# Attention: the split of the maxima moved ahead of the pieces' subtraction on GpSimd, their transposes a step earlier, and the loops written out

## The reference, cut to what matters

```python
x = x + 0.5 * ffn(layernorm(x))        # 8 experts, one for each token, with a capacity
x = x + attn(layernorm(x))             # the part that the change is in
x = x + 0.5 * ffn(layernorm(x))

def attn(x):                           # 16 heads of 8 numbers, causal
    q, k, v = split(sn_dense(x, W_qkv), 3)
    att = where(causal == 0, big_neg, einsum('bhqd,bhkd->bhqk', q, k) * hd ** -0.5)
    att = softmax(att, axis=-1)
    x = einsum('bhqk,bhkd->bhqd', att, v)
    return sn_dense(x, W_proj)
# ffn: num = x @ waff.T (the router's product), softmax, argmax and rank choose the
# expert; then gelu(x @ W1 + b1) @ W2 + b2 of that expert
```

## Time and profile before

| | |
|---|---|
| median of 3 runs | 1170.29 us (1165.38 to 1170.43) |
| the profiled execution's own time | 1164.83 us |
| its span, first to last instruction | 1163.0 us |
| granted clock of TensorE, mean | 0.875 of full speed |
| turns 0 to 31 of the attention | from about 376 us to about 885 us of the span |
| one pass of the loop, four turns | 63.9 us |

### The profile page before, as it was taken

The page is one execution under the profiler, slowest core; times in us unless marked ns, Lnnn a source line. Parts: engine busy times, 40 slices in busy tenths (PEclk is TensorE's granted clock), DMA queues, the critical chain, the costliest instruction groups (busy, mean ns, idle before and its releaser), DMA issues. The chain is left out here.

```text
span 1163.0 us, 28246 instructions
## 1 busy us (share of the span) xinstructions
PE 913.6 (79%) x8020; PEld 690.2 (59%) x8054; DVE 708.6 (61%) x2090; ACT 591.6 (51%) x1538; POOL 721.1 (62%) x1170
## 2 busy tenths in 40 slices
PE   2485638999936899999999999999984455988776
PEld 1374218999923566666666566656552134977776
DVE  6487954444326577777777777777753983434331
ACT  3023415666612566666666666666662433654543
POOL 4261976444132677677776777777652596777775
PEclk9655558999967999999999999999996556999998
DMA  5261002222216455544555544455410001212121
GB/s 163 82 170 43 0 8 66 66 69 67 51 46 119 88 105 117 117 103 105 107 108 117 109 103 104 107 116 115 98 40 10 1 0 38 52 51 53 48 50 30
DMA packets 124656, 88.51 MB, mean 76 GB/s; under 512 B 13649, under 2 KB 115078, under 8 KB 124566
## 3 DMA queue, kind: packets, MB, share of 16 engines
q1 hardware_dynamic: 101782, 52.36, 20.1%
q0 software_dynamic: 8960, 18.14, 6.6%
q10 hardware_dynamic: 13824, 16.92, 6.6%
HBM read 52.23 MB, written 34.87 MB: 75 GB/s over the span
## 5 line engine op out<-in xcount | busy, mean ns | idle before, releaser
L1379 DVE TENSOR_REDUCE at_mx<-at_pp 128x2 f32<-128x512 f32 (+1 forms) x384 | 259.8, 686 | 80.0 <-PE at_pp L1233 68.9
L1165 ACT ACTIVATE at_pt<-at_pm 128x512 f32<-128x512 f32 x384 | 224.4, 598 | 150.1 <-PE at_pm L1244 81.3
L1108 POOL TENSOR_SCALAR_AFFINE_SELECT at_pt<-at_pt 128x256 f32<-128x256 f32 (+1 forms) x384 | 182.1, 490 | 125.9 <-ACT at_pt L1165 121.5
L855 ACT ACTIVATE e_ht<-e_ps_h,b1t 128x128 f32<-128x128 f32 x576 | 164.8, 372 | 120.5 <-PE e_ps_h L883 120.4
L817 POOL DMA_INDIRECT e_x<-rows,gidx x144 | 139.0, 965 | 94.5 <-DVE e_y L935 48.3
L883 PE MATMUL e_ps_h<-e_xnt,e_w1own 128*128 128x128 f32 x1152 | 158.1, 282 | 27.8 <-issue 22.7
L883 PEld LDWEIGHTS e_ps_h<-e_xnt,e_w1own 128*128 128x128 f32 x1152 | 144.2, 197 | 31.9 <-issue 31.9
L893 PE MATMUL e_ps_y<-w,e_ht 128*128 x1152 | 159.7, 282 | 0.0
L893 PEld LDWEIGHTS e_ps_y<-w,e_ht 128*128 128x128 f32 x1152 | 140.5, 192 | 1.7
L1244 PE MATMUL at_pm<-qs,kb 128*128 128x256 bf16 x512 | 97.7, 272 | 29.0 <-ACT at_pt L1165 26.2
L935 DVE SCALAR_TENSOR_TENSOR e_y<-e_ps_y,e_x 128x256 f32<-128x256 f32 x72 | 30.6, 425 | 143.2 <-PE e_ps_y L893 143.2
(11 more groups left out here) (256 smaller groups left out, 1626.2 us busy)
## 6 DMA issues: line engine op xcount, KB each, us to landing
at_qkd<-at_part SPq DMA_DIRECT2D x64, 192.0 KB, 3.0
kb<-at_qkd SPq DMA_DIRECT2D x64, 96.0 KB
qs<-at_qkd ACTq DMA_DIRECT2D x64, 96.0 KB
x<-e_y SPq DMA_DIRECT2D x36, 128.0 KB, 1.8
rows<-ts_x ACTq DMA_DIRECT2D x16, 264.0 KB, 3.0
rows<-at_x SPq DMA_DIRECT2D x32, 132.0 KB
ts_x<-in_x_dram SPq DMA_DIRECT2D x16, 256.0 KB, 3.2
x_by_token<-at_xa SPq DMA_DIRECT2D x32, 128.0 KB
```

Source lines behind the costliest of these rows:

```text
L855: last = a.activation(hid_t[j % NB][:, f, :], ps_h[j % NB][:, f, :], ACT.Gelu, bias=c.b1t[:, ds(e, 1), f])
L1108: g.affine_select(out=tile, in_=tile, compare_op=ALU.is_ge, fill=0.0, base=0, pattern=[[0, n], [1, P]], channel_multiplier=-1).then_inc(ma ...
L1165: a.activation(pt[u % RING][:, :], pm[u % 2], ACT.Exp, scale=SCALE).then_inc(exped, 1)
L1379: v.tensor_reduce(out, src, axis=AX.X, op=ALU.max).then_inc(maxed, 1)
```

## The change

It has three parts.

1. On GpSimd, in step 5, the four operations that cut the maxima of sequence b+1 come ahead of the subtraction for sequence b+3; before, they came behind it.
2. On TensorE the maxima are turned in step 7 instead of step 8, and the router's product is made in step 8 instead of step 7. ScalarE's copies follow: the turned maxima in step 7 and the router's numbers in step 8. The waits on the shared bank are changed to match: the transposes wait for the product of the turn before, and the product waits for the copy of the turned maxima.
3. All turns of the attention and all steps of `token_stats` are written out. The loops go, and with them the registers and the increments of a semaphore `passed`.

The diff, cut to its core:

```diff
-        def turns(turn):
-            for b in range(-4, NQ):
-                turn(b, b % NQ, lambda o, b=b: 0 <= b + o < B)
-            yield
-            for b in range(B - NQ, B + 2):
-                turn(b, b % NQ, lambda o, b=b: 0 <= b + o < B)
-            yield
-        def run(eng, turn):
-            emit = turns(turn)
-            next(emit)
-            with eng.Fori(1, B // NQ - 1) as i:
-                for k in range(NQ):
-                    turn(i * NQ + k, k, lambda o: True)
-            next(emit)
+        def run(turn):
+            for b in range(-4, B + 2):
+                turn(b, b % NQ, lambda o, b=b: 0 <= b + o < B)
...
 # GpSimd, step 5
+                    if u == 5 and has(1):
+                        n, q = b + 1, (k + 1) % 2
+                        wait(pool, maxed, (n + 1) * NP)
+                        flat = mx[q][:, :, :, :].rearrange("p j r g -> p j (r g)")
+                        g.tensor_copy(mp[q][:, :, 0, :], flat).then_inc(cuts, 1)
...
+                        g.tensor_tensor(mp[q][:, :, 2, :], nr[q][:, :, :], mp[q][:, :, 1, :], ALU.subtract).then_inc(mp_done, 1)
                     if u == 5 and has(3):
                         q = (k + 1) % 2
                         wait(pool, b_done, b + 4)
                         g.tensor_tensor(part[q][:, 2:4, :], rest[q][:, :].rearrange("p (a n) -> p a n", a=2), part[q][:, 1:5:3, :],
                                         ALU.subtract).then_inc(part_done, 1)
-                    if u == 5 and has(1):
-                        n, q = b + 1, (k + 1) % 2
-                        wait(pool, maxed, (n + 1) * NP)
...
 # ScalarE
-                    if u == 7 and has(-2):
-                        wait(act, num_mm, b - 1)
...
-                    if u == 8 and has(1):
+                    if u == 7 and has(1):
                         q = (k + 1) % NQ
                         wait(act, mt_tr, b + 2)
...
+                    if u == 8 and has(-2):
+                        wait(act, num_mm, b - 1)
...
 # TensorE
-                    if u == 7 and has(-2):
-                        wait(pe, x2t_out, b - 1)
-                        wait(pe, v_out, b + 4, B)
...
+                    if u == 7 and has(1):
+                        wait(pe, mp_done, b + 2)
+                        wait(pe, v_out, b + 4, B)
+                        wait(pe, num_out, b - 2)
...
+                    if u == 8 and has(-2):
+                        wait(pe, x2t_out, b - 1)
+                        wait(pe, mt_out, b + 2, B)
...
-                    if u == 8 and has(1):
-                        wait(pe, mp_done, b + 2)
-                        wait(pe, v_out, b + 4, B)
-                        wait(pe, num_out, b - 1)
```

More of the change, by code:

```diff
@@ L361, in wait, with run @@
         def wait(eng, s, n):
-            if not isinstance(n, int) or n > 0:
+            if n > 0:
                 eng.wait_ge(s, n)
[L366 to L374, removed]
+        def run(step):
+            for b in range(NB):
+                step(b, b % NX, b == 0, b == NB - 1)
         @blk.sync
@@ L378, in load @@
             def load(b, k, first, last):
-                if not isinstance(b, int) or b >= NX:
+                if b >= NX:
                     sp.wait_ge(x_out[k], (b - k) * (16 // NX))
-                    sp.sem_inc(passed, 1)
                     sp.wait_ge(xn_done, (b - (NX - 1)) * TS)
-                    sp.sem_inc(passed, 1)
                     sp.wait_ge(xnorm_done, b - (NX - 1))
-                    sp.sem_inc(passed, 1)
                 sp.dma_start(x_row[k][:, :, 0:D], x_v[:, ds(b, 1), :, :]).then_inc(x_in[k], 16)
-            run(sp, load)
+            run(load)
         @blk.gpsimd
@@ L404, in roots @@
                 g.tensor_tensor(c.xnorm[:, ds(b * TS, TS)], x_row[k][:, :, D + 1], x_row[k][:, :, D + 2], ALU.mult).then_inc(xnorm_done, 1)
-            run(pool, roots)
+            run(roots)
         @blk.scalar
@@ L424, in step @@
                     numbers(b, k)
-            run(act, step)
+            run(step)
             for k in range(NX):
@@ L459, in step @@
                 norm(b, k)
-            run(dve, step)
+            run(step)
         @blk.tensor
@@ L482, in step @@
                     project(b, k)
-            run(pe, step)
+            run(step)
 def consts(nc, m):
@@ L1018, in wait @@
         def wait(eng, s, n, most=None):
[L1020 to L1024, removed]
+            n = n if most is None else min(n, most)
+            if n > 0:
+                eng.wait_ge(s, n)
         def dma_count(b, slots, each=1):
@@ L1085, in turn @@
                     sp.dma_start(row_v[:, ds(b - 2, 1), :, :], x2[k % 2][:, :, :]).then_inc(row_out[k % 2], 16)
-            run(sp, turn)
+            run(turn)
             for k in range(2):
@@ L1130, in turn @@
                         g.tensor_tensor(c.xnorm[:, ds(n * TPB, TPB)], x2[q][:, :, D + 1], x2[q][:, :, D + 2], ALU.mult).then_inc(xnorm_done, 1)
+                    if u == 5 and has(1):
[3 more added lines that the diff above has]
+                        g.tensor_copy(mp[q][:, :, 0, :], flat).then_inc(cuts, 1)
+                        wait(pool, cuts, n * 3 + 1)
+                        g.tensor_tensor(nr[q][:, :, :], flat, mp[q][:, :, 0, :], ALU.subtract).then_inc(cuts, 1)
+                        wait(pool, cuts, n * 3 + 2)
+                        g.tensor_copy(mp[q][:, :, 1, :], nr[q][:, :, :]).then_inc(cuts, 1)
+                        wait(pool, cuts, n * 3 + 3)
+                        g.tensor_tensor(mp[q][:, :, 2, :], nr[q][:, :, :], mp[q][:, :, 1, :], ALU.subtract).then_inc(mp_done, 1)
                     if u == 5 and has(3):
@@ L1151, in turn @@
                         g.tensor_tensor(xa[k % 2][:, :, D + 1], vare[k % 2][:, :], mhalf[:, :], ALU.pow).then_inc(rstd1, 1)
-            run(pool, turn)
+            run(turn)
         @blk.scalar
@@ L1211, in turn @@
                             act.dma_start(qs[q][to:to + size, :, :], src[48 * r:48 * r + size, :, :]).then_inc(qk_in[q], 16)
-            run(act, turn)
+            run(turn)
         @blk.tensor
@@ L1272, in small @@
                         wait(pe, xn_done, (b + 4) * TPB)
[L1273 to L1275 removed]
+                        wait(pe, num_out, b - 2)
+                        wait(pe, v_out, b + 3)
                         for j in range(TPB):
@@ L1307, in small @@
                         last.then_inc(otr, 1)
+                    if u == 7 and has(1):
+                        wait(pe, mp_done, b + 2)
+                        wait(pe, v_out, b + 4, B)
+                        wait(pe, num_out, b - 2)
+                        for j in range(TPB):
+                            last = te.transpose(mi[0].bitcast(BF16)[0:3 * H, j * P:(j + 1) * P],
+                                                mp[(k + 1) % 2][:, j, :, :].rearrange("p t h -> p (t h)"), c.identb[:, :])
+                        last.then_inc(mt_tr, 1)
+                    if u == 8 and has(-2):
+                        wait(pe, x2t_out, b - 1)
+                        wait(pe, mt_out, b + 2, B)
+                        for j in range(TPB):
+                            last = te.matmul(mi[0][:, j * E:(j + 1) * E], x2t[k % 2][:, j * P:(j + 1) * P], c.waff_t[:, :],
+                                             start=True, stop=True)
+                        last.then_inc(num_mm, 1)
                     if u == 7 and has(-1):
@@ L1339, in turn @@
                     small(u)
-            run(pe, turn)
+            run(turn)
         @blk.vector
@@ L1422, in turn @@
                         statistics(b - 1, x2[q], bn2[q], vare2[q], bnd2, mv2, var2, True)
-            run(dve, turn)
+            run(turn)
 def macaron(nc, io, out):
```

35 lines of the change are left out of this document (2 added, 33 removed).

## The result

The changed kernel takes 1203.45 us (median of 4 runs, 1194.41 to 1207.01), the kernel before 1168.74 us (4 runs, 1165.38 to 1170.43). The ratio is 1.0286 with an interval of 1.0257 to 1.0316: slower by 34.7 us. The forecast was 1200 us, with +32.6 us against the profiled execution. Profile against profile it is 1203.77 - 1164.83 = +38.9 us; the span is 1201.7 us.

The account below looks back on a forecast made before the run. The prediction took a circle through GpSimd's subtraction and the landing of `at_qkd` as the bound; +36.0 + 0 - 0.7 - 6.7 + 4 + 0 = +32.6 us gave 1197.4 us, or 1202.9 by the median; it said 1200, range 1186 to 1210.

Parts of the forecast that it names:

- The circle through the subtraction: Attention turn, 15.98 us: GpSimd's queue, subtraction, `at_qkd` flight, ScalarE's transfers, exponential and TensorE's tile by key, without slack.
- The cuts at full price: GpSimd step 5: cuts ahead delay the subtraction by 1.20 us in each of 30 turns, +36.0 us.
- TensorE's new waits at 0: TensorE steps 7 and 8: waits of 0.6 us a turn fit in the room; 18 us if not, chance 6%.
- Writing out at -6.7 us: Attention loop: written-out turns last 15.70 instead of 15.98 us, over 24 turns, mostly from SyncE's register work.
- The last turns at -0.7: Turns 30 and 31: earlier transfer of the turned maxima wins 0.5 to 1 us together, taken as -0.7.
- Fetches at +4 us: Written-out turns: instruction fetches meet some `at_qkd` flights at 0.4 us each, +4 us, bounds 0 and +10.
- The clock: TensorE: its clock would still be granted in full, and its longer wait costs nothing.
- two bases: Whole kernel: 1197.4 us from the profiled execution and 1202.9 us by the median of the runs.
- The signs named beforehand: Profile after: subtractions near 17.0 us apart, flight 3.6 to 4.0, TensorE's wait near 2 or split, ScalarE's gap about 1 longer.
- The rule on taken branches: Loop's five jumps back would each stall engines for a fetch, so writing out is preferred; the sum was left unchanged.

Follow-up runs that it names:

- spare operations: Kernel before plus four unused GpSimd operations of the cuts' size each turn: ratio 1.000 placed behind subtraction and cuts, 1.032 placed ahead of the subtraction.
- part 1 with filler: Kernel before with only the cuts moved ahead of the subtraction, in the loop, plus five extra TensorE products in step 0 of each turn: ratio 1.035.
- both moves: Kernel before with the cuts ahead of the subtraction and the maxima turned in step 7, product in step 8, loops kept: ratio 1.032.
- the cuts behind: Changed kernel with GpSimd's order as before, subtraction first, still written out and maxima turned in step 7: ratio 1.016.
- part 3 alone: Kernel before with all turns written out, cuts still behind the subtraction and maxima turned in step 8: ratio 0.998.
- part 1 alone: Kernel before with only the four cuts moved ahead of the subtraction, loops kept: ratio 1.061.
- the spare operations ahead: Kernel before plus four unused GpSimd operations of the cuts' size ahead of the subtraction each turn, cuts still behind it: ratio 1.032.

## Why the prediction was right, and which of its terms were off

**The circle through the subtraction** is right. It was read from two engines that start on different work at one moment. The spare operations show that the place in GpSimd's queue decides, and part 1 with filler that a later subtraction alone costs its delay.

**The cuts at full price.** Forecast 1.20 us a turn; the block measures 1.10 in the written-out kernel, and in the loop the turn grew by 1.24 (both moves) and 1.11 (spare operations). Right. For the turn ahead of turn 0 the first exponential came 1.4 us earlier in the span instead of 1.2 later, since the attention began 2.3 us earlier; the cost was there (+0.9) but a gain in the written-out stages ahead, which I had put at 0, covered it.

**TensorE's new waits at 0.** Right where the cuts come first: the product waits 2.5 us in 15 turns, and the transposes not measurably (in the loop with both moves 3.8 us in 10 turns). It doesn't hold as such: with the cuts behind they are the bound (17.15 us a turn).

**Writing out at -6.7 us.** Too small for undisturbed turns, -12.4 with the rest. Against the loop with both moves such a turn is 0.65 us shorter: SyncE starts 0.31 us sooner, the subtraction stands 0.25 us nearer to the first exponential, and 0.09 is spread. But with the order as before writing out shortened nothing (16.06 us a turn), as the next circle was met.

**The last turns at -0.7.** The wait for the turned maxima's transfer at turn 31 (1.21 us before) is gone, but turns 28 to 30 took 1.3 us more. No run shows the term by itself.

**Fetches at +4 us** were mis-sized. In the changed kernel all seven flights over 4.9 us (of 29) had a fetch of 16 KB 2.6 to 3.4 us after the send-off, and the flights without any took 3.72 to 3.75 us. A smaller one, of 8 KB at 3.2 us, cost 0.1, and one of 16 KB at 3.5 us nothing. The moment alone doesn't decide: with part 3 alone fetches of 16 KB at 3.2 to 3.5 us cost between 0 and 1.9 us. Turn 28 before, from which the 0.4 was taken, was a mild case, and turn 0, at 5.5 us, was in the trace and not used. Measured: +9.3 us.

**The clock** is the step that was missing. I wrote that a longer wait of TensorE costs nothing, and that the clock would still be granted in full. With part 1 alone the lowered clock cost 1.6 us a turn, more than the cuts themselves. Here up to 7.6 us in turns 4 to 27 stand beside it. The length of one wait doesn't decide alone: in turns 4 to 28 of the changed kernel five waits of 2.27 to 2.31 us left the clock up, those of 2.60 and 2.51 had half clock beside them, and with part 1 alone waits of 2.0 to 2.1 us, one in every turn, were enough. The trace before had it all in turns 0 and 1: the fetch, the long flight, the long wait, the half clock.

**That the total fell inside the range** is in part luck. Profile against profile it missed by 6.3 us (+38.9 instead of +32.6), and 1200 was set between two bases. The fetches and what is left beside the clock (+14 together beyond the forecast) stood against a larger gain from writing out, a block of 1.10 and the early start.

**The signs named beforehand.** The subtractions follow each other at 16.7 us (near 17.0), the undisturbed flight is 3.74 us, and both reads start together: as said. TensorE's wait at the first tile by key is 0.95 and 1.14 us behind the undisturbed turns 10 and 11, not near 2. ScalarE's gap between steps 9 and 10 grew by 0.18 us, not 1, while the wait ahead of step 9 grew by 0.64: the delay had reached the steps before. The clock wasn't granted in full.

**The rule on taken branches**, weighed beside part 3 (the Trainium skill, Runtime: NRT & Kernel Launch, section "Instruction fetch mechanics"), gets no support here: writing out alone gave 0.998 (0.995 to 1.001). In the loop no long flight occurred behind the first pass. That the loop saved in fetches about what its registers cost fits this but wasn't measured apart.

## What to carry to other kernels

Follow the one late wait of a turn back to where two engines start together, and look at what stands in the queue ahead of its producer: a microsecond there costs a microsecond a turn, and behind it nothing. When such a circle is shortened or an operation is taken forward, look for the circles within half a microsecond of it (here the turned maxima's transfer and `kb`, which share SyncE's queue), since they cap the gain at once. And mind how TensorE's idle time is cut up. With part 1 alone it waited 2.0 us a turn in one place and the half clock kept coming back; with the spare operations ahead it waited 1.1 and 0.9 us in two places and the clock held.

## What was not expected of the hardware

A chain with little slack and a clock that follows activity feed each other: in the run with part 1 alone the half clock came back every 17 to 21 us through the whole loop, 89 us of it in 24 turns, and 1.1 us of useless products a turn took 1.6 us off each turn. In six turns of the changed kernel's 4 to 27 a single fetch of 16 KB of instructions stood beside a delay of 1.2 to 1.7 us of a transfer of 384 KB that SyncE and ScalarE waited for. In the loop kernels `at_qkd` was there within 3.8 us in all of turns 8 to 27.
